# A chip-resident transformer block on Trainium2: cross-attention scores in two half-precision parts instead of rounded single precision, and weights turned one stage earlier

## What is computed

```python
x = x + jnp.tanh(g_xattn[0]) * _L0_xattn_ref(_layernorm(x), ctx_2048, mask_BxS2_bk0)
x = x + jnp.tanh(g_ffn[0]) * _L0_ffn_ref(_layernorm(x), L0_ffn_w_up, L0_ffn_w_down)
x = x + jnp.tanh(g_xattn[1]) * _L1_xattn_ref(_layernorm(x), ctx_2048)
x = x + jnp.tanh(g_ffn[1]) * _L1_ffn_ref(_layernorm(x), weight1, weight2, weight3)

# _L1_xattn_ref(qkv, y): 16 heads of ch = 32 channels
k = v = y.reshape(bs * N_HEADS, ch, -1)
scale = 1.0 / math.sqrt(math.sqrt(ch))
weight = jnp.einsum('bct,bcs->bts', q * scale, k * scale)
weight = jax.nn.softmax(weight, axis=-1)
a = jnp.einsum('bts,bcs->bct', weight, v)
```

## Time and profile before

| | us |
|---|---|
| median of 3 runs (1840.54 to 1844.35) | 1842.4 |
| the profiled execution | 1841.3 |
| its span in the profile | 1839.5 |
| stage A | 0 to 453 |
| stage B | 453 to 686 |
| stage C | 686 to 1564 |
| stage D | 1564 to 1839.5 |

### The profile page before, as it was taken

How to read it: one execution, slowest core, us unless ns; L and a number is a source line. 1 busy time by engine, 2 the same in 40 slices (tenths; PEclk the granted TensorE clock), 3 DMA queues, 4 the chain that set the end, 5 groups by cost and what they waited for, 6 DMA issues and landing times. The chain is left out here.

```text
span 1839.5 us, 22129 instructions
## 1 busy us (share of the span) xinstructions
PE 1658.9 (90%) x7540; PEld 800.2 (44%) x7568; DVE 1147.0 (62%) x1529; ACT 760.9 (41%) x1241; POOL 843.0 (46%) x340
## 2 busy tenths in 40 slices
PE   5999999898777876899999999899999997799898
PEld 2454444444433333444444444444444432344443
DVE  3669989884455557676766676667676630444543
ACT  1321211211543431566666666566666665111110
POOL 0022234544221125577778888677777877000000
PEclk9999999899899995999999999999999999799999
DMA  8232223322111115444333334444433310400000
GB/s 320 80 120 77 83 93 96 103 100 79 39 30 35 34 41 137 113 114 112 77 96 89 98 97 113 114 113 113 113 88 90 77 46 1 95 23 0 23 23 23
DMA packets 134316, 152.57 MB, mean 83 GB/s; under 512 B 59694, under 2 KB 101826, under 8 KB 134214
## 3 DMA queue, kind: packets, MB, share of 16 engines
q1 hardware_dynamic: 129222, 140.76, 29.3%
q10 hardware_dynamic: 4992, 10.49, 1.7%
HBM read 73.42 MB, written 10.76 MB: 46 GB/s over the span
## 5 line engine op out<-in xcount | busy, mean ns | idle before, releaser
L1352 DVE TENSOR_REDUCE c_piece_max<-c_unit 128x1 f32<-128x804 f32 x512 | 485.0, 984 | 241.0 <-PE c_unit L1490 238.4
L1448 ACT ACTIVATE c_prob<-c_scores 128x512 f32<-128x512 f32 (+1 forms) x832 | 473.3, 596 | 267.3 <-PE c_scores L1507 250.5
L1287 POOL TENSOR_TENSOR c_prob_sum<-c_prob_sum,c_prob 128x2048 f32<-128x2048 f32 x96 | 439.4, 4577 | 12.0 <-ACT c_prob L1448 6.0
L1507 PE MATMUL c_scores<-c_queries,c_keys 98*128 98x512 f32 (+1 forms) x832 | 354.8, 443 | 32.7 <-ACT c_prob L1448 17.4
L1490 PE MATMUL c_unit<-c_khigh,c_qdiag 128*128 128x402 f32 x1024 | 303.2, 381 | 20.1 <-DMA c_qdiag<-c_qhigh 10.1
L1490 PEld LDWEIGHTS c_unit<-c_khigh,c_qdiag 128*128 128x128 f32 x1024 | 186.6, 198 | 150.1 <-DVE c_piece_max L1352 90.1
L1507 PEld LDWEIGHTS c_scores<-c_queries,c_keys 98*128 98x128 f32 (+1 forms) x832 | 152.4, 186 | 202.0 <-ACT c_prob L1448 141.3
L1516 PE MATMUL c_out<-c_prob,c_VT 128*32 128x512 f32 (+1 forms) x1664 | 220.8, 610 | 0.0
L641 PE MATMUL a_S<-a_ctxT,a_xnT 128*128 128x401 f32 x512 | 190.7, 517 | 7.2 <-ACT a_prob L598 3.9
L671 PE MATMUL a_o<-a_ctx,a_probT 128*128 128x512 f32 (+1 forms) x416 | 181.2, 592 | 0.0
L1287 POOL TENSOR_TENSOR c_prob_sum<-c_prob 128x2048 f32<-128x2048 f32 x16 | 73.5, 4592 | 121.1 <-ACT c_prob L1448 121.1
(11 more groups left out here) (196 smaller groups left out, 1975.0 us busy)
## 6 DMA issues: line engine op xcount, KB each, us to landing
c_keys<-c_khigh SPq DMA_DIRECT2D x128, 200.2 KB, 3.0
c_k<-in_keys SPq DMA_DIRECT2D x16, 801.0 KB, 6.3
c_keys<-c_k SPq DMA_DIRECT2D x64, 200.2 KB, 3.0
a_ctx<-in_ctx SPq DMA_DIRECT2D x12, 1024.0 KB, 6.8
c_VT<-in_values SPq DMA_DIRECT2D x16, 768.0 KB
a_ctxT<-in_ctxT SPq DMA_DIRECT2D x12, 802.0 KB, 4.7
c_queries<-c_qhigh SPq DMA_DIRECT2D x128, 64.0 KB, 2.6
a_weights<-in_L_ffn_weight SPq DMA_DIRECT2D x3, 1408.0 KB, 14.7
```

The lines of the kernel that those rows point to most:

```text
L1287: nc.gpsimd.tensor_tensor(psum4[:], a[:], prob[(j * MC + c) % RING][:], ALU.add).then_inc(sums_taken, 2 if i == 1 else 1)
L1352: nc.vector.tensor_reduce(piece_max[j % 2][:, k // 2, k % 2:k % 2 + 1], U[bank(unit)][:, :, 0:PIECE], axis=AX.XY, op=ALU.max).then_inc(uni ...
L1448: nc.scalar.activation(prob[(j * MC + c) % RING][0:w, h, :], STp[h % 2][0:w, :], ACT.Exp, scale=SCALE).then_inc(exp_done, 1)
L1507: nc.tensor.matmul(STp[h % 2][0:w, :], K[p][:, h, c * P:c * P + w].bitcast(F32R), Q[p][:, h, :].bitcast(F32R), start=True, stop=True).then ...
```

## The change

In stage C the parts of keys and queries become F16 (16 bits) in place of F32R. For their range the keys are multiplied by a factor (`key_scale`) that brings the largest number of the context to 2 to the 13, and the exponential's scale becomes that factor's inverse with the old scale in it (`score_scale`), a column in SBUF instead of a constant. The maxima are one row against a row of 512s instead of two against ones: 97 rows in the stack, and `high_of_maxima` and `rest_of_maxima` are gone. `rest_of_k` moves from the end of POOL's slot to DVE, into the stream of units, and writes a tile of its own (c_krest).

The factor needs the largest number of the context: stage A gets `context_top` on DVE after tiles 2, 6, 10 and 14, a reduction over all of `CT`, a round trip through memory by SP to spread the result over the partitions, and `context_scales` behind `add_out` of tile 14. SP's loads of the next `CT` wait for these reductions.

The turned weights of D get their place ahead of C, and SP issues the three transfers in C behind its last slot, not at the start of D. SBUF has room for them since the stacks are half as wide.

```diff
@@ stage A
+            def context_top(b):
+                for n in range(4):
+                    dve.wait_ge(ctxT_loaded[n], 16 * (b + 1))
+                nc.vector.tensor_reduce(ctx_tops[:, b:b + 1], CT[:], axis=AX.XY, op=ALU.max, apply_absolute_value=True).then_inc(ctx_topped, 1)
+                if b == B - 1:
+                    dve.wait_ge(ctx_topped, B)
+                    nc.vector.tensor_reduce(ctx_tops[:, B:B + 1], ctx_tops[:, 0:B], axis=AX.X, op=ALU.max).then_inc(ctx_topped, 1)
+
+            def context_scales():
+                dve.wait_ge(ctx_top_loaded, 16)
...
+                steps.did(nc.vector.reciprocal(scales[:, 0:1], scales[:, 3:4]))
+                steps.did(nc.vector.tensor_scalar(scales[:, 1:2], scales[:, 3:4], KEY_SCALE, None, ALU.mult))
@@ maximum(k) and add_out(k - 2)
+                if k % ST == 2:
+                    context_top(k // ST)
@@ stage A, SP
             def load_transposed(b):
+                if b > 0:
+                    sp.wait_ge(ctx_topped, b)
...
+            sp.wait_ge(ctx_topped, B + 1)
+            sp.dma_start(flat_ctx_top.rearrange("(p o) -> p o", o=1), ctx_tops[:, B:B + 1]).then_inc(ctx_top_out, 16)
@@ stage C, tiles
-        KA = KM + 2
+        KA = KM + 1
+        ONES = 2.0 ** 9
-        krest = [k[:].bitcast(F32R) for k in kt]
-        khigh = [sb(f"c_khigh{j}", [P, MK], F32R) for j in range(2)]
+        krest = [sb(f"c_krest{j}", [P, MK], F16) for j in range(2)]
+        khigh = [sb(f"c_khigh{j}", [P, MK], F16) for j in range(2)]
-        K = [sb(f"c_keys{j}", [KA, H, MK]) for j in range(2)]
-        Q = [sb(f"c_queries{j}", [KA, H, D]) for j in range(2)]
+        K = [sb(f"c_keys{j}", [KA, H, MK], F16) for j in range(2)]
+        Q = [sb(f"c_queries{j}", [KA, H, D], F16) for j in range(2)]
@@ stage C, POOL
-            def rest_of_k(n, j):
-                pool.wait_ge(khigh_ready, n + 1)
-                nc.gpsimd.tensor_tensor(krest[j], kt[j][:], khigh[j][:], ALU.subtract).then_inc(rests_ready, 1)
-
-            def rest_of_maxima(n):
-                pool.wait_ge(nhigh_ready, n + 1)
...
                 add_up(g, j, 5)
-                if nxt:
-                    rest_of_maxima(g + 1)
                 add_up(g, j, 6)
...
                     rest_of_q(g + 2, j % 2)
-                    rest_of_k(g + 2, j % 2)
@@ stage C, DVE
+            def rest_of_k(n, j):
+                dve.wait_ge(khigh_ready, n + 1)
+                wait(dve, stacked, (n - 1) * STACKS)
+                nc.vector.scalar_tensor_tensor(krest[j][:], kt[j][:], key_scale, khigh[j][:], ALU.mult, ALU.subtract).then_inc(krest_ready, 1)
@@ slot: behind the maximum of a pair
+                    if main and more and unit[2:] == (j + 2, 6):
+                        rest_of_k(g + 2, j % 2)
@@ stage C, ACT
-                nc.scalar.copy(khigh[j][:], kt[j][:]).then_inc(khigh_ready, 1)
+                nc.scalar.activation(khigh[j][:], kt[j][:], ACT.Copy, scale=key_scale).then_inc(khigh_ready, 1)
-                    nc.scalar.activation(prob[(j * MC + c) % RING][0:w, h, :], STp[h % 2][0:w, :], ACT.Exp, scale=SCALE).then_inc(exp_done, 1)
+                    nc.scalar.activation(prob[(j * MC + c) % RING][0:w, h, :], STp[h % 2][0:w, :], ACT.Exp, scale=score_scale[0:w]).then_inc(exp_done, 1)
@@ stage C, PE
             def rows(unit):
-                pe.wait_ge(nparts_ready, n + 1)
+                pe.wait_ge(nmax_ready, n + 1)
@@ stage C, SP
             every_slot(sp, slot)
+            for k in range(3):
+                sp.dma_start_transpose(shared["turned_weights"][k][:], weights_dram[k]).then_inc(shared["turned_loaded"][k], 16)
@@ stage D, SP
-            sp.wait_ge(shared["weights_stored"], 48)
-            for k in range(3):
-                out = w12T[k] if k < 2 else w3T
-                sp.dma_start_transpose(out[:], weights_dram[k]).then_inc(w_loaded[k], 16)
```

More of the change, by code:

```diff
@@ L1074, in cross_attention_1 @@
         kt = [sb(f"c_k{j}", [P, MK]) for j in range(2)]
[L1075 to L1076 removed]
+        krest = [sb(f"c_krest{j}", [P, MK], F16) for j in range(2)]
+        khigh = [sb(f"c_khigh{j}", [P, MK], F16) for j in range(2)]
         xn = sb("c_xn", [P, D])
[L1078 to L1082 removed]
+        qhigh = [sb(f"c_qhigh{j}", [P, D], F16) for j in range(2)]
+        qrest = sb("c_qrest", [P, D], F16)
+        QZ = [sb(f"c_qdiag{j}", [P, H, D], F16) for j in range(2)]
+        K = [sb(f"c_keys{j}", [KA, H, MK], F16) for j in range(2)]
+        Q = [sb(f"c_queries{j}", [KA, H, D], F16) for j in range(2)]
         VT = [sb(f"c_VT{j}", [P, MC, P]) for j in range(2)]
@@ L1095, in cross_attention_1 @@
         piece_max = [sb(f"c_piece_max{j}", [P, H * TB, 2]) for j in range(2)]
-        nmax = sb("c_nmax", [P, H, TB])
-        nparts = sb("c_nparts", [P, TB, H, 2])
-        nrow = sb("c_nrow", [2 * H, D], F32R)
+        nmax = sb("c_nmax", [P, TB, H])
+        nrow = sb("c_nrow", [H, D], F16)
         rden = sb("c_rden", [P, D])
@@ L1291, in _ @@
             rest_of_q(0, 0)
-            rest_of_k(0, 0)
             steps.link(pool.memset(QZ[1][:], 0.0))
@@ L1361, in keep_rows @@
                 dve.wait_ge(unit_full, FULL0 + rows_place(n) + 1)
-                nc.vector.tensor_copy(nrow[:], U[bank(unit)][0:2 * H, 0, :]).then_inc(unit_read, 1)
+                nc.vector.tensor_scalar(nrow[:], U[bank(unit)][0:H, 0, :], 1.0 / ONES, None, ALU.mult).then_inc(unit_read, 1)
                 dve.wait_ge(unit_read, UNITS0 + rows_place(n) + 1)
@@ L1374, in _ @@
             statistics(1)
+            rest_of_k(0, 0)
             def slot(g, j, main, nxt, more, later):
@@ L1424, in split_queries @@
                 nc.scalar.copy(qhigh[j][:], xn[:]).then_inc(qhigh_ready, 1)
-            def high_of_maxima(n):
-                act.wait_ge(nmax_ready, n + 1)
-                wait(act, unit_full, FULL0 + rows_place(n - 1) + 1 if not isinstance(n, int) or n > 0 else 0)
-                nc.scalar.copy(nparts[:].bitcast(F32R)[:, :, :, 0].rearrange("p t h -> p h t"), nmax[:]).then_inc(nhigh_ready, 1)
             def take_out(g):
@@ L1465, in slot @@
                         split_keys(g + 2, j % 2)
-                    if c == (8 if not isinstance(g, int) or g > 0 else 10) and nxt:
-                        high_of_maxima(g + 1)
                 if nxt:
@@ L1489, in pair @@
                     at = STARTS[2 * half + e]
-                    last = nc.tensor.matmul(U[bank(unit)][:, e, 0:PIECE], QZ[o][:, h, t * P:(t + 1) * P].bitcast(F32R), khigh[o][:, at:at + PIECE], start=True, stop=True)
+                    last = nc.tensor.matmul(U[bank(unit)][:, e, 0:PIECE], QZ[o][:, h, t * P:(t + 1) * P], khigh[o][:, at:at + PIECE], start=True, stop=True)
                 last.then_inc(unit_full, 1)
@@ L1494, in rows @@
                 n = unit[1]
-                pe.wait_ge(nparts_ready, n + 1)
+                pe.wait_ge(nmax_ready, n + 1)
                 pe.wait_ge(unit_read, rows_place(n) + 1)
                 for t in range(TB):
-                    last = nc.tensor.transpose(U[bank(unit)][0:2 * H, 0, t * P:(t + 1) * P], nparts[:, t, :, :].rearrange("p h a -> p (h a)"), ident[:])
+                    last = nc.tensor.transpose(U[bank(unit)][0:H, 0, t * P:(t + 1) * P], nmax[:, t, :], ident[:])
                 last.then_inc(unit_full, 1)
@@ L1506, in score @@
                 pe.wait_ge(exp_done, g * EXPS + H * c + h + 1)
-                nc.tensor.matmul(STp[h % 2][0:w, :], K[p][:, h, c * P:c * P + w].bitcast(F32R), Q[p][:, h, :].bitcast(F32R), start=True, stop=True).then_inc(scores_ready, 1)
+                nc.tensor.matmul(STp[h % 2][0:w, :], K[p][:, h, c * P:c * P + w], Q[p][:, h, :], start=True, stop=True).then_inc(scores_ready, 1)
             def out(g, j, c):
@@ L1609, in ffn_1 @@
         FC = F // P
-        w12T = [sb(f"d_w{k + 1}T", [P, DC, F], BF16) for k in range(2)]
-        w3T = sb("d_w3T", [P, FC, D], BF16)
+        *w12T, w3T = shared["turned_weights"]
         nhalf = sb("d_nhalf", [P, ST])
@@ L1628, in ffn_1 @@
         O = [ps(f"d_o{t}", [P, 512]) for t in range(ST)]
-        w_loaded = [sem(f"d_w{k}_loaded") for k in range(3)]
+        w_loaded = shared["turned_loaded"]
         consts_ready = sem("d_consts_ready")
@@ L1815, in program @@
         weight_tops, bit_scales = weight_stats[:, 0:2], weight_stats[:, 2:4]
+        ctx_scales = stack.enter_context(nc.sbuf_tensor("ctx_scales", [P, 4], F32))
         gates = stack.enter_context(nc.sbuf_tensor("gates", [P, 4], F32))
@@ L1855, in program @@
         if "C" in stages:
-            cross_attention_1(nc, shared, keys, values)
+            turned = [[P, DC, w.shape[0]] for w in weights[:2]] + [[P, weights[2].shape[1] // P, D]]
+            shared["turned_weights"] = [stack.enter_context(nc.sbuf_tensor(f"turned_weights{k}", t, BF16)) for k, t in enumerate(turned)]
+            shared["turned_loaded"] = [sem(f"turned_loaded{k}") for k in range(3)]
+            cross_attention_1(nc, shared, keys, values, weights)
         if "D" in stages:
```

57 lines of the change are left out of this document (33 added, 24 removed).

## The result

The changed kernel takes 1873.6 us (four runs, 1872.8 to 1874.4) against 1841.9 for the kernel before: a ratio of 1.0171, 95% interval 1.0153 to 1.0188, so 1.7% slower. The forecast was 1865, slower by 1.2%, with a range up to 1893. The direction and the two mechanisms that carry it were right; 8.6 us are missing, and three terms of the sum were off.

A forecast was written before the change was run, and what follows sets the result against it. It took C's chunks as rings in TensorE's in-order queue, where inserted waits count in full. 1841.3 + 11.8 - 4.8 + 21.0 - 2.4 - 2.6 = 1864.3, plus 1.1 for the median: 1865 us, range 1822 to 1893.

The forecast's parts named there:

- the two mechanisms that carry it: rest_of_k blocked by POOL's addition in C, +1.5 us a group; context reductions lengthening TensorE's chain in stage A, +11.8.
- stage A: Four context reductions on VectorE lengthen a chain TensorE waits for: +8.3 at the third, +3.5 at the fourth, +11.8 us.
- entry of C: Start of C: smaller gaps between unit pairs (-2.2) and transposes waiting for the maxima alone (-2.6), together -4.8 us.
- groups: Stage C: 14 groups with rest_of_k at +1.5 us each (+21.0), the two last at -1.2 each (-2.4).
- entry of D: Start of D: turned weights are there before the stage, so TensorE waits less: -2.6 us.
- a ring: A chunk in C: scores, exponentials, scores, outputs, with units filling gaps; savings count only in the ring, waits between units fully.
- The F16 term: Stage C: weight loads 0.093 us shorter against exponentials 0.091 longer, -0.09 a chunk, -1.2 us a group.
- The block: rest_of_k on VectorE stands until POOL's addition, sharing SBUF ports, ends: about 3.8 us long, TensorE's unit load 2.2 late.
- The clock: Rival in C's groups: the new 2 us pause lowers the granted clock, 14 x 2.1 = 29 more, 1894 us; chance 0.13.
- The first rival: Groups of C: rest_of_k meets a free POOL, so F16's saving is kept: 1828 us; chance 0.18.

The follow-up runs named there:

- rest_of_k out of the way: The changed kernel with rest_of_k back at the end of POOL's slot and keys not scaled: 1820.4 us, 48.8 us a group.
- the experiment: The changed kernel with rest_of_k on POOL, its three turned weight loads issued at the start of stage D again: 1823.1 us against 1820.4 with early loads.
- 1827.1: The changed kernel with rest_of_k still on VectorE, but behind the twelfth pair of the group instead of the seventh: 1827.1 us, ratio 0.9927 to before.
- 1829.6: The changed kernel with the last two of POOL's seven additions of a group cut to 8 of 512 columns: 1829.6 us, ratio 0.9940 to before.

## Why the prediction was right, and where it was off

The sum had five terms, of which the groups' 21.0 and -2.4 are one here. In the profiled execution, with A's end at the start of B (453.4 before, 469.7 after), C's entry up to its first exponential, the groups from there to the last taking of the output (819.7 before, 842.2 after), and all behind that put down to D's entry:

| term | forecast | measured |
|---|---|---|
| stage A | +11.8 | +16.2 |
| entry of C | -4.8 | -5.9 |
| groups | +18.6 | +22.5 |
| entry of D | -2.6 | +0.3 |
| stage B (not in the sum) | 0 | -0.2 |

**What bounds the kernel.** Right. A group is a ring with TensorE's queue in order; savings of TensorE's busy time counted only in part, and one wait between two units counted in full.

**The F16 term** (-1.2 a group) measured -1.5 with rest_of_k out of the way. The group with units and without rest_of_k fell from 47.8 to 46.6, the last, without units, only from 47.8 to 47.6: where there are no unit loads, shorter score loads and longer exponentials about cancel. That is the working in the ring, by which two exposed score loads (-0.19) stand against two exponentials (+0.18).

**The block**, taken from the two rows of stage A, was right in kind and close in size: 4.57 us long where 3.8 were named, 2.9 of waiting for POOL and 1.7 of its own. It was longer because rest_of_k came 1.7 us into POOL's addition and not 2.5. What the block costs by itself is 51.06 less 48.8, 2.3 us; the forecast had 1.5 and the 1.2 saved, 2.7. With F16's 1.5 a group at full clock is 0.8 longer than before, not 1.5: over the thirteen windows 11.0 instead of 19.5.

**The clock** was a rival, priced at 2.1 us a group and given 0.13, and I took it as all or nothing. It came behind ten of the fourteen pauses and cost some 1.8 each, 17.5 together, where the sum had 0. The step that failed is the one that left the clock behind pauses of 2 us, of which the groups at full clock in the trace of before had none, out of the forecast because the shorter ones were harmless. By luck, two things kept the groups' term near its number all the same: the smaller block, and the loop's turn, whose window took 55.90 before and 53.03 now, which is 3.7 less than its block would make it. The two last groups gave 1.4 instead of 2.4, and the first, up to its taking, 0.9 less than before: 11.0 + 17.5 - 3.7 - 1.4 - 0.9 = 22.5. So the term of 18.6 was nearer to 22.5 than its parts were to theirs, and that is no merit of the working.

**Stage A** was mis-sized by 4.4, in two places. At tile 12 the chain was 10.0 late, not 8.3: of the second reduction more was left than the 1.5 computed from VectorE's idle time. The idle time ahead of the maximum of tile 9, 3.41 us before, was not all there to absorb it, since the scores that it waits for came later as well:

```profile
268.14 1.83 DVE L464 TENSOR_REDUCE a_nmax<-a_S 128x1 f32<-128x1604 f32 x1 [1.97 <-PE a_S L679]
```

So 1.97 of it stayed idle, and the maximum of tile 10 is 3.3 late. The end went as forecast up to ACT's copy: it comes at 452.96 instead of 439.45, 13.5 late, 3.5 more than the 10.0. The other 2.7 are TensorE's clock, which the sum had at nothing here too. While TensorE waited its 4.29 us the granted clock fell, for 6.8 us, and the last block of outputs takes 13.6 us where it took 11.3:

```profile
452.40:459.20 6.80, 5.60 (x11) 3.02 (x12) 0.00 (x0) 1.82 (x4) 6.43 (x3) 0.50 0.11 39
454.70:468.30 13.60, 13.59 (x28) 5.64 (x26) 0.00 (x0) 0.74 (x2) 4.13 (x2) 0.83 0.06 19
```

All five other kernels in which that wait is 4.3 us long have the low stretch at this place (452 to 453 us). The five in which it is 1.1 us or less, the kernel before among them, have none before stage A ends.

**The entry of C**, with the two small steps on the maxima gone, was close. The transposes now wait 1.31 us for the maxima alone, as worked out; the other 3.3 of the 5.9 were forecast at 2.2.

```profile
742.70 1.01 PE L1521 MATMUL c_unit<-ident,c_nmax 128*4 128x128 f32 x4 [1.31 <-DVE c_nmax L1377]
```

**The entry of D** was right by the experiment (2.7 to 3.2 us) and hidden in the changed kernel's profile by the two low stretches.

**The first rival** (POOL free, 1828) did not come true in the change, and it is what two of the experiments produced on purpose: 1827.1 and 1829.6.
